# Expert stages of a four-layer gated cross-attention kernel: router split across the first expert steps, last sums joined in PSUM, shared expert written as token rows

## What is computed

```python
# layer 1: one expert of eight for each token
scores = feats @ centroids.T
onehot = one_hot(argmax(scores))                         # E = 8
alpha  = sigmoid(score of the chosen expert)
ys     = for each expert: h = layernorm(xs)*g + b; xs + relu(h @ W1e.T + b1e) @ W2e.T + b2e  # F = 512
out    = alpha * (onehot . ys) + (1 - alpha) * feats
# layer 3: two experts of eight for each token, and a shared one
scores  = softmax(xt @ gate_w.T)
combine = (one_hot(top_k(scores, 2)) * top_k weights).sum
y       = sum over experts of combine_e * (silu(xt @ gate_k) * (xt @ up_k)) @ down_k  # F = 512
shared  = silu(xt @ sh_gate) * (xt @ sh_up) @ sh_down                                 # FS = 256
x       = x + tanh(g_ffn[3]) * (y + shared)
```

## Time and profile before

| what | value |
|---|---|
| runs | 844.13, 853.32 and 854.43 us, median 853.32 |
| the profiled execution, its own time | 846.48 us |
| its span, first to last instruction | 844.6 us |
| mean granted TensorE clock | 0.975 of 2.4 GHz |
| PE busy | 772.2 us (91%) |
| DVE busy | 612.8 us (73%) |
| ACT busy | 451.9 us (53%) |
| POOL busy | 197.1 us (23%) |

### The profile page before, as it was taken

The page is one execution under the profiler, slowest core; times in us unless marked ns, Lnnn a source line. Parts: engine busy times, 40 slices in busy tenths (PEclk is TensorE's granted clock), DMA queues, the critical chain, the costliest instruction groups (busy, mean ns, idle before and its releaser), DMA issues. The chain is left out here.

```text
span 844.6 us, 14259 instructions
## 1 busy us (share of the span) xinstructions
PE 772.2 (91%) x5234; PEld 552.9 (65%) x5234; DVE 612.8 (73%) x1159; ACT 451.9 (53%) x681; POOL 197.1 (23%) x163
## 2 busy tenths in 40 slices
PE   6998789989999999999899887899998889999996
PEld 4654556656677777777676546666776767777774
DVE  6678586677666477888777877776655877778876
ACT  4466352146656407999825755565554245555553
POOL 3000020024635420222220001246355101111112
PEclk9999799999999998999999999999999989999999
DMA  9100000130230200000270000002301000000000
GB/s 346 71 2 1 2 0 1 70 130 1 53 76 2 51 2 1 1 0 1 100 317 2 1 2 1 2 1 52 77 8 45 1 1 1 0 1 0 0 1 25
DMA packets 3948, 30.55 MB, mean 36 GB/s; under 512 B 592, under 2 KB 944, under 8 KB 2352
## 3 DMA queue, kind: packets, MB, share of 16 engines
q1 hardware_dynamic: 3888, 29.73, 10.4%
HBM read 29.10 MB, written 0.62 MB: 35 GB/s over the span
## 5 line engine op out<-in xcount | busy, mean ns | idle before, releaser
L187 PE MATMUL banks<-normed_t_high,work_split 128*128 128x512 f32 x250 | 109.5, 438 | 10.4 <-DVE work_split L1152 4.4
L1091 POOL TENSOR_TENSOR work<-work 128x512 f32<-128x512 f32 x64 | 86.1, 1356 | 122.0 <-ACT work L1053 122.0
L189 PE MATMUL banks<-normed_t_high,work_split 128*128 128x512 f32 x250 | 100.9, 404 | 0.0
L188 PE MATMUL banks<-normed_t_low,work_split 128*128 128x512 f32 x250 | 100.6, 403 | 0.0
L713 DVE TENSOR_REDUCE work<-banks 128x2 f32<-128x512 f32 x128 | 84.4, 687 | 17.8 <-PE banks L455 15.4
L1828 ACT ACTIVATE work<-banks 128x512 f32<-128x512 f32 x68 | 40.7, 598 | 71.6 <-PE banks L189 71.6
L276 POOL TENSOR_TENSOR ln_rstd<-ln_var_eps,minus_half_and_newton 128x4 f32<-128x4 f32 x16 | 17.1, 1072 | 249.4 <-DVE ln_var_eps L242 240.7
L1941 DVE TENSOR_TENSOR work<-work,banks 128x512 f32<-128x512 f32 x68 | 46.6, 686 | 35.2 <-ACT work L1828 34.7
L187 PE MATMUL banks<-work_split 128*128 128x512 f32 x148 | 63.9, 432 | 6.2 <-DVE work_split L1904 4.8
L187 PEld LDWEIGHTS banks<-normed_t_high,work_split 128*128 128x128 f32 x250 | 47.9, 192 | 32.4 <-issue 17.0
L911 PE MATMUL banks<-work 128*64 128x256 f32 x512 | 65.0, 393 | 2.7 <-ACT work L1053 2.3
(11 more groups left out here) (290 smaller groups left out, 1737.2 us busy)
## 6 DMA issues: line engine op xcount, KB each, us to landing
raw_b<-in_wf SPq DMA_DIRECT2D x1, 6528.0 KB, 19.2
raw_a<-in_wf SPq DMA_DIRECT2D x1, 4096.0 KB, 13.4
raw_b<-reciprocal_rows SPq DMA_DIRECT2D x6, 512.0 KB, 6.1
raw_a<-reciprocal_rows SPq DMA_DIRECT2D x6, 512.0 KB, 6.4
raw_a<-in_wf SPq DMA_DIRECT2D x1, 2048.0 KB, 14.5
raw_b<-in_wb SPq DMA_DIRECT2D x1, 2048.0 KB, 18.6
raw_a<-in_wb SPq DMA_DIRECT2D x1, 2048.0 KB, 7.6
small_operands<-in_small SPq DMA_DIRECT2D x1, 1386.0 KB, 10.5
```

Source lines behind the costliest of these rows:

```text
L187: nc.tensor.matmul(o, w[0], m[0], start=start, stop=False)
L188: nc.tensor.matmul(o, w[0], m[1], start=False, stop=False)
L189: return nc.tensor.matmul(o, w[1], m[0], start=False, stop=stop)
L1091: nc.gpsimd.tensor_tensor(w_ps[g % 2].rearrange("p (h q) -> p h q", h=2), v[:, :, 0, :], v[:, :, 1, :], ALU.add).then_inc(W["ps"].sem, 1)
```

## The change

Both expert stages:

- `stack_pe` moves one step later on PE in f1 (between `up(3)` and `down(1)`) and two steps later in f3 (between `up(4)` and `down(2)`). `stack_act` moves from step 2 to step 4 in f1, and from step 1 to step 4 in f3. In f1's first pass the spreading matmuls and the copy of their result come one step later.
- f1's DVE: `step(0, 0)` is issued before the factors are formed (`factors`, six instructions), `step(0, 1)` after.
- f3's DVE: the first choice is found, then `step(0, 0)`, then three instructions of the second choice (`second_equal`), `step(0, 1)`, four more (`pick_first`), `step(0, 2)`, and then the factors (four instructions).
- f1's end: POOL no longer adds the last tile (`g_t[1]` of the last pass). PE forms the second half's token rows with `to_tokens`: plain float32 matmuls against the identity, first of `out_t`, then of `g_t[1]`, summed in bank 7.
- f3's end: the shared expert's `down` is turned round. For each of four tiles of 128 tokens it takes the activation tile as the stationary operand and 128 columns of weights as the moving one, so its output is token rows in bank 6 or 7; a `down` has 12 matmuls of 128 columns in place of 3 of 512. `to_tokens` adds the sum over experts to the same bank. The two copies (L1912), POOL's last two additions and `back_pe` are gone.

```diff
         nc.vector.tensor_tensor(half(lo, h), src, half(hi, h).bitcast(F32), ALU.subtract).then_inc(s_xs, 1)
-def back_pe(pe, ready, k):
-    for h in range(2):
-        pe.wait_ge(ready.sem, ready.at(0, E // 2, k + h - 1))
-        for t in range(4):
-            last = nc.tensor.transpose(ps[:, 6 + h, t * P:(t + 1) * P],
-                                       out_t[:, (4 * h + t) * P:(4 * h + t + 1) * P], ident)
-        last.then_inc(s_rt, 1)
+def to_tokens(src, k, first, last):
+    for t in range(4):
+        ins = nc.tensor.matmul(ps[:, k, t * P:(t + 1) * P], src[:, t * P:(t + 1) * P], ident,
+                               start=first and t == 0, stop=last and t == 3)
+    return ins
 def tokens_half(src, w, h):
     for t in range(4):
...
     order.wait()
-def pick_max(order, oh, s, t1, m):
+def pick_equal(order, s, t1, m):
     order.step(nc.vector.tensor_reduce(m, s, AX.X, ALU.max))
     mb = m.unsqueeze(2).to_broadcast((P, NT, E))
     order.step(nc.vector.tensor_tensor(t1, s, mb, ALU.is_equal))
+def pick_first(order, oh, t1):
     iota = col("iota").unsqueeze(1).to_broadcast((P, NT, E))
     order.step(nc.vector.tensor_scalar(t1, t1, -float(E), None, ALU.mult))
     order.step(nc.vector.tensor_tensor(t1, t1, iota, ALU.add))
     order.step(nc.vector.tensor_reduce(m2col, t1, AX.X, ALU.min))
     order.step(nc.vector.tensor_tensor(oh, t1, m2col.unsqueeze(2).to_broadcast((P, NT, E)), ALU.is_equal))
+def pick_max(order, oh, s, t1, m):
+    pick_equal(order, s, t1, m)
+    pick_first(order, oh, t1)
 def split_stack(order, w, at, last=False):
...
         for n in range(16):
             if n + 2 < 16 or not last_pass:
                 up(i, n + 2)
-            if n == 0 and stacked is not None:
+            if n == 1 and stacked is not None:
                 stacked()
-            if n % 8 == 2:
+            if n % 8 == (3 if stacked is not None and n < 8 else 2):
                 s = n // 8
                 at("cc", s)
                 pe.wait_ge(s_wt, 2)
...
     up(0, 0)
     up(0, 1)
     passes(pe, body, lambda: stack_pe(pe, 1, 5))
-    back_pe(pe, G["acc"], 0)
+    pe.wait_ge(G["acc"].sem, G["acc"].at(0, PASSES, -1))
+    for t in range(4):
+        last = nc.tensor.transpose(ps[:, 6, t * P:(t + 1) * P], out_t[:, t * P:(t + 1) * P], ident)
+    last.then_inc(s_rt, 1)
+    to_tokens(half(out_t, 1), 7, True, False)
+    pe.wait_ge(G["t"].sem, G["t"].at(0, PASSES, 0))
+    to_tokens(g_t[1], 7, False, True).then_inc(s_rt, 1)
 def f1_act(act):
     softmax_act(act, 1, scale=-1.0)
...
             at("up", n + 1)
             at("al", n - 3)
             at("dn", n - 3)
-            if n == 2 and stacked is not None:
+            if n == 4 and stacked is not None:
                 stacked()
             b, hidden = g_b1[s][:, f:f + 1], bank((0, 1, 2, 7)[n % 4])
             nc.scalar.activation(g_af[n % 4], hidden, ACT.Relu, bias=b).then_inc(s_act, 1)
             nc.scalar.activation(g_a[n % 4][0], hidden, ACT.Relu, bias=b).then_inc(G["a"].sem, 1)
-            if n % 8 == 4:
+            if n % 8 == (5 if stacked is not None and n < 8 else 4):
                 at("cb", s + 1)
                 at("t", 2 * s)
                 nc.scalar.activation(g_cw, bank(5, 2), ACT.Copy).then_inc(G["cc"].sem, 1)
...
 def f1_pool(pool):
     def body(i, last_pass):
-        for n in range(4):
+        for n in range(3 if last_pass else 4):
             h = n % 2
             pool.wait_ge(G["t"].sem, G["t"].at(0, i, n + 1))
             pool.wait_ge(G["acc"].sem, G["acc"].at(0, i, n - 1))
             nc.gpsimd.tensor_tensor(half(out_t, h), half(out_t, h), g_t[h], ALU.add).then_inc(G["acc"].sem, 1)
     passes(pool, body)
+    pool.wait_ge(G["t"].sem, G["t"].at(0, PASSES, 0))
 def f1_piece(dve, i, s, k):
...
     pick_max(order, oh, lg, t1, mcol)
     nc.vector.tensor_copy(lg, mcol.unsqueeze(2).to_broadcast((P, NT, E))).then_inc(s_lx, 1)
-    dve.wait_ge(s_le, 2)
-    order.step(nc.vector.tensor_scalar(ex, ex, 1.0, None, ALU.add))
-    order.step(nc.vector.reciprocal(ex, ex))
-    order.step(nc.vector.tensor_tensor(ex, ex, oh, ALU.mult))
-    dve.wait_ge(s_clear, 1)
-    split_stack(order, ex, 0, True)
+    def factors():
+        dve.wait_ge(s_le, 2)
+        order.step(nc.vector.tensor_scalar(ex, ex, 1.0, None, ALU.add))
+        order.step(nc.vector.reciprocal(ex, ex))
+        order.step(nc.vector.tensor_tensor(ex, ex, oh, ALU.mult))
+        dve.wait_ge(s_clear, 1)
+        split_stack(order, ex, 0, True)
     def step(i, n, last_pass=False):
         def at(name, k):
...
         nc.vector.scalar_tensor_tensor(out=g_t[h], in0=bank(3 + h), scalar=b2, in1=half(g_cw, h),
                                        op0=ALU.add, op1=ALU.mult).then_inc(G["t"].sem, 1)
     step(0, 0)
+    factors()
     step(0, 1)
     passes(dve, body)
...
         def down(n):
             s, h, f, nf = steps[n]
             at("al", n + 1)
+            c0 = (2 * nf + f) * P
+            if shared:
+                for t in range(4):
+                    tile = slice(t * P, (t + 1) * P)
+                    last = mm3(ps[:, 6 + h, tile], [v[:, tile] for v in k_a[n % 2]], [v[:, c0:c0 + P] for v in k_w[s]],
+                               start=f == 0 and t == 0, stop=False)
+                last.then_inc(K["dn"].sem, 1)
+                return
             if f == 0:
                 at("t", 2 * s + h - 1)
-            c0 = (2 * nf + f) * P
             mm3(bank(4 + h), [v[:, c0:c0 + P] for v in k_w[s]], k_a[n % 2], start=f == 0, stop=f == nf - 1)\
                 .then_inc(K["dn"].sem, 1)
         for n in range(len(steps)):
             if n + 2 < len(steps) or not shared:
                 up(i, n + 2, shared or (last_pass and n + 2 >= 16))
-            if n == 0 and stacked:
+            if n == 2 and stacked:
                 stack_pe(pe, 2)
             if n % 8 == 3 and not shared:
                 s = n // 8
...
                 for h in range(2):
                     last = nc.tensor.matmul(bank(6 + h), k_sel[s], half(k_wt, h), start=True, stop=True)
                 last.then_inc(K["cb"].sem, 1)
+            if shared and n == 0:
+                pe.wait_ge(K["cc"].sem, K["cc"].at(0, PASSES, 0))
             down(n)
+            if shared and n % 2:
+                h = n // 2
+                pe.wait_ge(K["acc"].sem, K["acc"].at(0, PASSES, h - 1))
+                to_tokens(half(out_t, h), 6 + h, False, True).then_inc(s_rt, 1)
     up(0, 0)
     up(0, 1)
...
         body(i, False, False)
     body(PASSES - 1, True, False)
     body(PASSES, True, True)
-    back_pe(pe, K["acc"], 2)
 def f3_act(act):
     softmax_act(act, 2)
...
         for n in range(1, 20 if last_pass else 17):
             gates(i, n)
             high(i, n - 1)
-            if n == 1 and stacked is not None:
+            if n == 4 and stacked is not None:
                 stacked()
             if n % 8 == 5:
                 s = n // 8
...
     with pool.Fori(0, PASSES) as i:
         body(i, 4)
-    body(PASSES, 2)
 def f3_piece(dve, i, s, k):
     w = raw_b[:, bass.ds(i * (2 * W_F3) + s * W_F3, W_F3)]
...
     softmax_dve(dve, order, 2)
     pick_max(order, oh, ex, t1, mcol)
-    order.step(nc.vector.scalar_tensor_tensor(out=lg.rearrange("p t e -> p (t e)"), in0=oh.rearrange("p t e -> p (t e)"),
-                                              scalar=-2.0, in1=ex.rearrange("p t e -> p (t e)"),
-                                              op0=ALU.mult, op1=ALU.add))
-    pick_max(order, oh2, lg, t1, mcol)
-    order.step(nc.vector.tensor_tensor(oh, oh, oh2, ALU.add))
-    order.step(nc.vector.tensor_tensor(ex, ex, oh, ALU.mult))
-    dve.wait_ge(s_clear, 2)
-    split_stack(order, ex, 0, True)
+    def second_equal():
+        order.step(nc.vector.scalar_tensor_tensor(out=lg.rearrange("p t e -> p (t e)"), in0=oh.rearrange("p t e -> p (t e)"),
+                                                  scalar=-2.0, in1=ex.rearrange("p t e -> p (t e)"),
+                                                  op0=ALU.mult, op1=ALU.add))
+        pick_equal(order, lg, t1, mcol)
+    def factors():
+        order.step(nc.vector.tensor_tensor(oh, oh, oh2, ALU.add))
+        order.step(nc.vector.tensor_tensor(ex, ex, oh, ALU.mult))
+        dve.wait_ge(s_clear, 2)
+        split_stack(order, ex, 0, True)
     def at(i, name, k):
         dve.wait_ge(K[name].sem, K[name].at(0, i, k))
...
     def weigh(i, q):
         h = q % 2
-        at(i, "dn", 4 * (q + 1) if q < 4 else 16 + 2 * (q - 3))
+        at(i, "dn", 4 * (q + 1))
         at(i, "acc", q - 1)
-        if q >= 4:
-            ins = nc.vector.tensor_copy(k_t[h], bank(4 + h))
-        else:
-            at(i, "cc", q // 2 + 1)
-            ins = nc.vector.tensor_tensor(k_t[h], bank(4 + h), half(k_cw, h), ALU.mult)
-        ins.then_inc(K["t"].sem, 1)
+        at(i, "cc", q // 2 + 1)
+        nc.vector.tensor_tensor(k_t[h], bank(4 + h), half(k_cw, h), ALU.mult).then_inc(K["t"].sem, 1)
     def next_weights(i, s, k, last_pass):
...
```

(11 more changed lines are left out.)

## The result

The new kernel takes 846.95 us, the median of 21 runs (841.11 to 849.32); the old one, in 21 runs beside it, 851.92 us (844.13 to 857.16). The ratio is 0.995, with a 95% interval from 0.9931 to 0.9969: about 4.3 us, or half a per cent, faster, and inside the 2% that the prediction takes for no change. The forecast was 846.7 us. Some executions of a kernel are over 1.5% longer than its fastest; the ratios, and the medians of the experiments, leave them out.

The account below looks back on a forecast made before the run. PE, busy 91% of the span, was taken as the bound, so only PE's work or waits count. Terms -3.1 + 0.8 + 0 - 0.9 = -3.2 us from 849.9 gave 846.7 us, range 839 to 855.

Parts of the forecast that it names:

- f3's first steps: Start of f3: `up(2)` no longer waits for the router and the clock's second fall goes, -3.1 us (-4.1 to -1.0).
- the clock's 1.65: f3's first steps: without PE standing still, no second fall of the granted clock; half of 3.3 us, 1.65, gained.
- f1's first steps: Start of f1: no wait to remove; a factors wait of 0.3 and a later `stack_act` cost +0.8 us (0 to +1.5).
- f1's end: End of f1: PE's wait for POOL's sum goes, but DVE needs the bank only later; 0 us (-0.3 to +0.5).
- f3's end: Shared expert's `down`: copies, POOL additions and transposes go, 48 narrow matmuls replace 12 wide ones; -0.9 us.
- 48p - 6.4: f3's end: its movement in us at pace p per narrow matmul; -1.9 at 0.093, nothing at 0.133, +4.6 at 0.23.
- Sum: All four places: -3.1 + 0.8 + 0 - 0.9 = -3.2 us.
- two pairs: Old kernel's four times, 844.1 and 846.5, 853.3 and 854.4; their middle, 849.9, was the forecast's base.
- the first (dear narrow matmuls): Rival at the shared expert's four `down`s: a narrow matmul costs up to 0.23 us; +2.3 us, 852.2; chance 0.27.
- The second (the wait only moves, and the clock falls anyway): Rival at f3's first steps: PE's wait moves to `down(0)` and `down(1)`; -1.1 us in all, 848.8; chance 0.17.
- The third (more than forecast): Rival: no new waits in f3, f1 costs nothing, narrow matmuls at 0.093 us; -6.0 us, 843.9; chance 0.11.
- The fourth (`stack_pe` still waits): Rival in f3: DVE reaches the factors late, so `stack_pe` waits; -1.9 in place of -3.1, 847.9; chance 0.05.

Follow-up runs that it names:

- Run 3: Old kernel with nine idle products between `up(1)` and `up(2)` of f3's first pass, router order unchanged: `up(0)` to `up(6)` 17.79 us in place of 19.0.
- run 5: New kernel with `stack_act` put ahead of step 4's waits in f1: `down(7)` at 15.56 us, `down(15)` at 98.26.
- run 6: New kernel with one unread POOL addition at f1's end: DVE's two additions 2.42 us, second residual addition 6.32 us after the last `down(15)`.
- run 1: Old kernel with only the new order of f3's first steps: 847.33 us against 851.28, ratio 0.9976; f3's end 9.57 us in place of 9.88.
- run 7: New kernel with the shared expert's `down` in plain float32: f3's end 6.94 us in place of 8.87; 839.44 us (4 runs), ratio 0.9855.

## Why the prediction came out

The time was nearly exact, 846.95 against 846.7, and the gain near, 4.3 us by the ratio against 3.2. That the time fits to 0.3 us is luck (see the scatter below). Step by step it was less even:

- f3's first steps: forecast -3.1, measured -3.79. The parts held: `up(2)` without a wait, no second fall of the clock, a new wait of 0.67 before `down(0)` (forecast 0.7). Two sizes were off. The wait of 0.3 before `down(1)` didn't come; and the old order had waits of its own behind `up(2)`, before `down(1)` among them, which I left out of the sum though they went too. The parts add up: 2.45 of waiting, 1.65 of clock and 0.37 of the old wait before `down(1)`, less the new 0.67, are 3.8. Run 3 shows what the clock's 1.65 needs: alone it gives 1.2 us, since DVE is then late by 0.45 more. The whole size holds for the first profile; with the low clock elsewhere it was 2.9 to 4.2.
- f1's first steps: forecast +0.8, measured +0.44 at `down(7)` and +0.57 over the stage (+0.27 to +0.57 in the other profiles). Sign and cause were right: the wait for the factors (none to 0.1 us in place of 0.3) was over-estimated, the place of ACT's copy is what costs (run 5).
- f1's end: forecast 0, bounds -0.3 to +0.5, measured -1.01. This step failed. "PE waits for POOL, but DVE doesn't need the bank yet" was right, and I stopped there. I read L1244's 2.41 us as the length of that work. 2.41 us for two additions of 512 columns should have stood out beside the 0.75 us of one in the next row, L351; POOL's addition at the same time held up the second of them by 1.0 us (run 6).
- f3's end: forecast -0.9, measured -1.01. The pace was taken from the rows as 0.115 us and is 0.112; the sum 48p - 6.4 gives -1.0 with it. Its 6.4 contains the 0.3 us of low clock in the old end, so at full clock the place is worth 0.7 (run 1). "Nothing there is paced under 0.12" was a misreading: 28 instructions in 3.39 us is duration by count, and the duration ends with the last one's own length of some 0.27 us. Start to start these plain float32 matmuls are 0.112 us apart too.
- Sum: -3.2 forecast, -5.2 by the distances. The two sizes and the missed step make up the difference: 0.7 + 0.2 + 1.0 + 0.1.
- The scatter: I took four times for two pairs, 844 to 846 and 853 to 854. With 21 runs there are no pairs, the times fill 844 to 857. The middle that I used, 849.9, lay 2 us under the old kernel's median, and that happened to make up for the gain that I had too small. All 21 times of the new kernel lie in the range of 839 to 855.

The rivals: the first (dear narrow matmuls) is refuted by the rows, 0.11 us against the 0.18 from which it would have decided. The second (the wait only moves, and the clock falls anyway) is refuted by 0.67 us in place of 2.45 and by 0.98 from 677 to 684. The third (more than forecast) came near in the size of f3's first steps, 3.79 of its 4.1, but not in its reason, for a new wait did come; elsewhere it failed. The fourth (`stack_pe` still waits) didn't happen. The figure of about 81 ns that the Trainium skill ("TensorE: Matmul & The Clock Gate", section "Back-to-back issue gap") gives for a sustained stream of 128 columns was not reached by the 128-column streams here: 0.11 us, for fp32r and for float32.

## What to carry to other kernels

Where an engine waits for a long chain of small instructions before its first step, put the first steps between the links: 2.45 us of waiting went, and the clock that would have fallen after it stayed. Before you call an edit free because its result isn't needed yet, look at who works beside it: ask of each neighbour whether its own duration is what its size predicts. Read a distance together with the clock inside it: the same order of the same work took 14.7 or 16.0 us. And a serial tail of narrow matmuls is counted in instructions, each some 0.11 us at 128 columns: a product in two instructions of plain float32 was the better form there than one in three of fp32r.

## What the runs showed of the hardware

- A narrow matmul (128 stationary columns, 128 moving) follows the one before at 0.112 us, in fp32r (the new kernel, 829.30 and 829.41) and in plain float32 (run 7, 16 from 834.49 to 836.28). fp32r with 256 moving columns stands at 0.12 (168.04, 168.16), so half the columns save next to nothing.
- DVE's addition with both inputs in SBUF takes 0.74 us alone; of two in a row beside one POOL addition of 1.70 us, the first took 0.74 and the second 1.76. Beside a POOL memset neither is slowed (old and new kernel, run 6).
- With PE at work through a wait of 2.45 us the granted clock stayed at 0.99 (run 3); standing still for 2.45 us, it fell to 0.51 soon after the earlier trace rows.
